# Selective-scan stage of a hybrid conv/attention network: carry handed to the scans by pointer, one pool of five state buffers, new orders on TensorE and ScalarE

## What is computed

```python
xs = jnp.stack([s0, s1, s0[..., ::-1], s1[..., ::-1]], axis=1)
x_dbl = jnp.einsum('bkdl,kcd->bkcl', xs, x_proj_w)
dts, bs, cs = (x_dbl[:, :, :R], x_dbl[:, :, R:R + N], x_dbl[:, :, R + N:])
dts = jnp.einsum('bkrl,kdr->bkdl', dts, dt_projs_w)
delta = jax.nn.softplus(dts + dt_projs_b[None, :, :, None])
def step(hst, inp):
    u_i, dt_i, b_i, c_i = inp
    dA = jnp.exp(dt_i[..., None] * A)
    hst = dA * hst + (dt_i * u_i)[..., None] * b_i[:, :, None, :]
    y = jnp.einsum('bkdn,bkn->bkd', hst, c_i)
    return (hst, y)
```

## Time and profile before

| what | value |
|---|---|
| median of 3 runs | 13091.68 us (13074.61 to 13094.74) |
| the profiled execution | 13113.0 us, span 13111.2 us |
| scan stage (first to last scan of VectorE) | 837.9 to about 11514 us |
| VectorE busy | 10558.8 us (81%) |
| GpSimd busy | 9200.7 us (70%) |
| TensorE busy, mean granted clock | 9546.4 us (73%), 0.816 |
| ScalarE busy | 9124.6 us (70%) |
| HBM | 148 GB/s over the span |

### The profile page before, as it was taken

One profiled execution on the slowest core, in us unless ns is written; L12 is line 12 of the kernel. 1 busy time (PEld: TensorE's weight loads), 2 busy tenths in 40 slices (PEclk: granted clock), 3 DMA queues, 4 the chain that ended last, 5 costly groups with the idle time before them and its releaser, 6 DMA issues. The chain is left out here.

```text
span 13111.2 us, 148286 instructions
## 1 busy us (share of the span) xinstructions
PE 9546.4 (73%) x34584; PEld 3395.6 (26%) x34584; DVE 10558.8 (81%) x6847; ACT 9124.6 (70%) x15557; POOL 9200.7 (70%) x3956
## 2 busy tenths in 40 slices
PE   8867676677777777766777776777767676669888
PEld 2322222222222222222222222222222222223333
DVE  6768888888888888888888888888888888866665
ACT  6767777777777777777777777777777777735555
POOL 0038888888888888888888888888888888822111
PEclk9977877778787877787878787888777888879998
DMA  3456666666666666666666666666666666644442
GB/s 101 127 138 159 158 161 160 163 160 159 153 159 163 161 156 160 158 162 160 163 156 161 159 155 163 161 160 157 159 161 160 163 163 163 160 109 104 102 101 52
DMA packets 577621, 1948.60 MB, mean 149 GB/s; under 512 B 106614, under 2 KB 111638, under 8 KB 562198
## 3 DMA queue, kind: packets, MB, share of 16 engines
q1 hardware_dynamic: 573714, 1938.65, 61.8%
q10 hardware_dynamic: 3076, 0.97, 0.0%
HBM read 1532.38 MB, written 406.85 MB: 148 GB/s over the span
## 5 line engine op out<-in xcount | busy, mean ns | idle before, releaser
L1057 POOL TENSOR_TENSOR dBu<-rep,shared 128x1024 f32<-128x1024 f32 x2304 | 5366.8, 2353 | 972.4 <-DMA rep<-dd_dram 866.6
L747 PE MATMUL py<-hC,fold 128*32 128x512 f32 x12288 | 2599.6, 766 | 1450.9 <-ACT y L917 1258.6
L1016 DVE TENSOR_TENSOR_SCAN pd<-pd,dBu 128x1024 f32<-128x1024 f32 x1536 | 3506.1, 2283 | 165.5 <-ACT dBu L851 138.7
L826 ACT ACTIVATE pd<-rep,a_now 128x1024 f32<-128x1024 f32 x2304 | 2560.9, 1112 | 354.4 <-DVE hC L1025 167.8
L1067 POOL TENSOR_TENSOR hC<-shared 128x1024 f32<-128x1024 f32 x768 | 1797.1, 2360 | 816.0 <-DVE shared L997 814.8
L1067 POOL TENSOR_TENSOR hC<-h,shared 128x1024 f32<-128x1024 f32 x768 | 1804.5, 2350 | 797.2 <-DVE h L1016 794.4
L1025 DVE TENSOR_TENSOR hC<-pd,shared 128x1024 f32<-128x1024 f32 x1536 | 1880.5, 1224 | 395.0 <-PE py L747 249.0
L1016 DVE TENSOR_TENSOR_SCAN h<-pd,dBu 128x1024 f32<-128x1024 f32 x768 | 1751.4, 2280 | 71.0 <-ACT dBu L851 49.1
L997 DVE TENSOR_TENSOR_SCAN shared<-shared,carry,pd 128x1024 f32<-128x1024 f32 x576 | 1319.2, 2330 | 522.9 <-PE pd L727 408.1
L883 ACT ACTIVATE shared<-shared,turned_b 128x192 f32<-128x192 f32 x4096 | 1551.7, 442 | 0.0
L747 PEld LDWEIGHTS py<-hC,fold 128*32 128x32 f32 x12288 | 493.9, 129 | 3262.0 <-issue 2957.0
(11 more groups left out here) (170 smaller groups left out, 12357.4 us busy)
## 6 DMA issues: line engine op xcount, KB each, us to landing
rep<-dd_dram SPq DMA_DIRECT2D x1024, 768.0 KB, 12.1
shared<-bc_dram SPq DMA_DIRECT2D x3584, 128.0 KB, 3.9
u<-u_dram SPq DMA_DIRECT2D x128, 768.0 KB, 5.8
dd_dram<-LG SPq DMA_DIRECT2D x256, 384.0 KB, 3.5
dd_dram<-RL SPq DMA_DIRECT2D x256, 384.0 KB, 3.7
y_dram<-y SPq DMA_DIRECT2D x256, 384.0 KB, 3.7
shared<-y_dram SPq DMA_DIRECT2D x63, 1536.0 KB, 16.0
u_dram<-shared SPq DMA_DIRECT2D x32, 1536.0 KB, 7.6
```

Source lines behind the costliest of these rows:

```text
L747: last = mm(py[32 * g:32 * g + 32, t2(t)], fold[:, :], hC[:, j % 2 * 3 + g, t2(t)], start=(j % 4 == 0), stop=(j % 4 == 3), skip_group_chec ...
L826: go(dst, rep[:, half, 0, g, :], ACT.Exp, scale=a_now[:, column(i)]).then_inc(S.exped, 1)
L1016: v.tensor_tensor_scan(turned(dst, k), turned(pd[:, i % 2, :], k), turned(dBu[:, ring(c, place(i)), :], k), 0.0, ALU.mult, ALU.add).then_i ...
L1057: nc.gpsimd.tensor_tensor(dBu[:, ring(c, p), :], rep[:, half, 1, g, :], BB[:, r, :], ALU.mult).then_inc(S.dbu, 1)
```

## The change

- All scans take `carry[:, i]` as their starting value; `fold_state`, 18 activations a chunk in three chunks of four, is gone with its semaphore.
- `hs` (3 places) and `h` (2) become one pool of five places for the 12 states that GpSimd weighs (`KEPT`), given out by the table `HOME`. A place is written when the tile that had it before has been weighed and saved.
- TensorE's order: `make_step(n + 2, 0)` now closes the body before (behind `make_x_dbl` and `turn_b`, ahead of reduce 7) where `make_step(n + 1, 0)` opened it; `add_up(n + 1, 0)` stands between reduce 0 and 1; `skip(n, 0)` moves from ahead of tile 9 to behind tile 14; reduce 2 stands between tiles 10 and 11; `make_step(n + 1, 1)` behind tile 14; reduce 6 ahead of `make_x_dbl`.
- ScalarE's tables are new: 12 steps of `scale_du` lie ahead in the chunk before (8 until now), `copy_b` moves to i = 23 of the chunk before, most steps of half 0 come one or two tiles earlier, `copy_y(n - 1, 1)` at i = 2, `copy_y(n, 0)` at i = 14, and `relu` and `one_plus` of half 1 right behind it.
- VectorE's `delta_u` moves from behind tiles 9 and 19 to behind tiles 10 and 20.
- `y` has one place for both halves, with one semaphore.

```diff
+        KEPT = tuple(i for i in range(NS) if TRIPLES[i // 3][1] == 3 or i % 3 == 2)
+        HOME = (0, 1, 2, 3, 4, 0, 1, 2, 3, 4, 2, 3)
...
+        def kept_before(n, i):
+            slot, at_slot = HOME[KEPT.index(i)], KEPT.index(i) - 1
+            while at_slot >= 0 and HOME[at_slot] != slot:
+                at_slot -= 1
...
@@ scan (VectorE)
+                    if is_kept(i):
+                        dve.wait_ge(S.hc_pool, done(weighed_pool(*kept_before(n, i))))
...
                 if c > 0:
-                    dve.wait_ge(S.folded, done(folds(bk, c, i)))
...
+                    dve.wait_ge(S.carried, done(carries(bk, c - 1, i)))
+                    first = carry[:, i:i + 1]
...
-                                     0.0, ALU.mult, ALU.add).then_inc(S.scanned, 1)
+                v.tensor_tensor_scan(turned(state(i), k), turned(decay, k), turned(drive, k),
+                                     first, ALU.mult, ALU.add).then_inc(S.scanned, 1)
@@ body (TensorE)
-                if left:
-                    make_step(n + 1, 0)
                 reduce_states(n, 0)
-                reduce_states(n, 1)
-                skip(n, s, 0)
                 if left:
                     add_up(n + 1, 0)
-                for i in (9, 10, 11):
-                    turn_back(bk, c, i)
+                reduce_states(n, 1)
+                turn_back(bk, c, 9)
+                turn_back(bk, c, 10)
                 reduce_states(n, 2)
+                turn_back(bk, c, 11)
                 turn_back(bk, c, 12)
                 if left:
                     turn_du(n + 1, 0)
                 turn_back(bk, c, 13)
+                turn_back(bk, c, 14)
                 if left:
                     make_step(n + 1, 1)
-                turn_back(bk, c, 14)
+                skip(n, s, 0)
                 reduce_states(n, 3)
...
                     turn_du(n + 1, 1)
+                reduce_states(n, 6)
                 if left >= 2:
                     make_x_dbl(n + 2, s)
-                reduce_states(n, 6)
-                if left >= 2:
                     turn_b(n + 2)
+                    make_step(n + 2, 0)
                 reduce_states(n, 7)
@@ tables and body (ScalarE)
-            AHEAD = 8
-            SCALE = {0: 4, 1: 3, 2: 3, 3: 1, 4: 2, 5: 3, 6: 4, 7: 4}
-            SCALE_NEXT = {21: 2, 22: 4, 23: 2}
+            SCALE = {0: 3, 1: 1, 3: 3, 4: 2, 5: 7, 6: 3, 7: 1}
+            SCALE_NEXT = {20: 3, 21: 3, 22: 1, 23: 5}
...
-                    if i + 2 < NS and c > 0 and not is_turned(i + 2):
-                        fold_state(bk, k, c, i + 2)
-                    elif i + 2 >= NS and c < NC - 1:
-                        fold_state(bk, k, c + 1, i + 2 - NS)
-                    if i == 3 and (c > 0 or k > 0):
+                    if i == 2 and (c > 0 or k > 0):
                         copy_y(n - 1, 1)
-                    if i == 15:
+                    if i == 14:
                         copy_y(n, 0)
```

More of the change, by code:

```diff
@@ L599, in store_y @@
                 sp.sem_inc(S.passed, 1)
-                sp.dma_start(a.y_flat[row, :, half, :], y[:, half, :]).then_inc(y_stored[half], 16)
+                sp.dma_start(a.y_flat[row, :, half, :], y[:, :]).then_inc(y_stored, 16)
             def load_first_y(n):
@@ L605, in load_first_y @@
                 sp.wait_ge(S.dbu_turned, done((n + 1) * TURNED))
-                for half in range(2):
-                    sp.wait_ge(y_stored[half], done(16 * K * NC))
+                sp.wait_ge(y_stored, done(32 * K * NC))
                 for k, sem in ((0, S.y_loaded0), (1, S.y_loaded1)):
@@ L660, in _ @@
             chunk_loop(sp, body)
-            for half in range(2):
-                sp.wait_ge(y_stored[half], done(16 * BK * NC))
+            sp.wait_ge(y_stored, done(32 * BK * NC))
         @block.tensor
@@ L717, in turn_back @@
                 n = bk * NC + c
[L718 to L723, removed]
+                pe.wait_ge(*freed(n, i))
+                if not is_kept(i - 2) and c < NC - 1:
+                    pe.wait_ge(S.carried, done(carries(bk, c, i - 2)))
                 for q in range(TB):
@@ L806, in expo @@
             def expo(bk, c, i):
-                n, i = at(bk * NC + c, i)
                 half, r, g = where(i)
+                n = bk * NC + c
                 if i % 12 == 0:
                     act.wait_ge(rep_loaded[half], done((n + 1) * 64))
[L811 to L819, removed]
-                else:
-                    if where(q)[1] < 3 and where(q)[2] < 2:
-                        act.wait_ge(S.hc_dve, done(weighed_dve(before, q)))
-                    else:
-                        act.wait_ge(S.scanned, done(scanned(before, q)))
+                if is_turned(i):
+                    act.wait_ge(S.hc_pool, done(weighed_pool(*kept_before(n, i))))
+                    for count in kept_carried(bk, c, i):
+                        act.wait_ge(S.carried, done(count))
+                    dst = kept(i)
+                else:
+                    act.wait_ge(*freed(n, i))
                     dst = pd[:, i % 2, :]
@@ L1016, in scan @@
-                v.tensor_tensor_scan(turned(dst, k), turned(pd[:, i % 2, :], k),
-                                     turned(dBu[:, ring(c, place(i)), :], k),
-                                     0.0, ALU.mult, ALU.add).then_inc(S.scanned, 1)
+                    decay, drive = kept(i), pd[:, i % 2, :]
+                else:
+                    dve.wait_ge(S.dbu, done(driven(n, place(i))))
+                    decay, drive = pd[:, i % 2, :], dBu[:, ring(c, place(i)), :]
+                    if is_kept(i):
+                        dve.wait_ge(S.hc_pool, done(weighed_pool(*kept_before(n, i))))
+                        for count in kept_carried(bk, c, i):
+                            dve.wait_ge(S.carried, done(count))
@@ L1034, in body @@
                 n, s = bk * NC + c, c % 2
-                for i in range(NS):
-                    scan(bk, k, c, i)
-                    if not is_turned(i) and i % 3 < 2:
-                        weigh(n, i)
-                    if i == 9 and left:
-                        delta_u(n + 1, 1 - s, 0)
-                    if i == 19 and left:
-                        delta_u(n + 1, 1 - s, 1)
+                for j in range(8):
+                    for i in range(3 * j, 3 * j + 3):
+                        scan(bk, k, c, i)
+                        if not is_kept(i):
+                            weigh(n, i)
+                        if left and i in (10, 20):
+                            delta_u(n + 1, 1 - s, (10, 20).index(i))
             chunk_loop(dve, body)
```

117 lines of the change are left out of this document (56 added, 61 removed).

## The result

The changed kernel takes 11,915.7 us (median of 4 runs, 11,912.25 to 11,927.4) against 13,093.2 for the kernel before (4 runs). The ratio is 0.9104, with a 95% interval of 0.9089 to 0.912. The forecast of 12,270 had the sign and lies 354 us too high; the measured time is inside the range and 81 us from rival (a), "nothing waits", which I had given 0.20. The gain was forecast at 6.3% and is 9.0%.

A forecast was written before the change was run, and what follows sets the result against it. VectorE was taken as the fullest engine, 71.0 us a chunk plus 12.4 of waits. Terms -187.8, -696.5, -314.4 (`copy_delta`), -249.0, +104, +64, +372, +84 sum to -824 us: 12,270 us, 6.3% faster; range 11,800 to 12,660.

The forecast's parts named there:

- rival (a): Nothing waits: TensorE stays fast and the late preparation chain and reduce 2 terms vanish; 11,835 us, chance 0.20.
- the pointer's +104: VectorE's scans: a carry by pointer instead of an immediate costs 60 ns in each of 1728 scans, +104 us.
- The waits that go: VectorE's waits for transposes, turned tiles' decays, delta copy, reduces and folds, each taken as an edit's target: 1447.7 us.
- Folds gone: VectorE's waits for ScalarE's folds all go, -187.8 us; the folds' own 607.4 us on ScalarE count nothing.
- Turned tiles: VectorE's waits for TensorE's transposes (629.1) and turned tiles' decays (67.4) go by new order and five places, -696.5 us.
- Reduce 2 ahead of tile 11: TensorE's reduce 2, newly ahead of tile 11's transposes, makes them late by 0.5 us a chunk, +64 us.
- Reduce 6: Placed ahead of `make_x_dbl` on TensorE, it no longer holds up the product of tile 0, -249.0 us.
- What is late next: Preparation chain round the chunk, from `copy_y` to `expo(3)`, makes scan 3 late by 3.0 us in 124 chunks, +372 us.
- Image ends: Reduce 7, queued behind `make_step`, delays ScalarE and SyncE's `load_rep`: 12 us at each of 7 image ends, +84 us.
- rival (d): Slower: TensorE falls to its low clock at the turned tiles, making later links late; 13,270 us, chance 0.05.
- Rival (b): GpSimd sets the pace, with 1 us of handing over in each of eight triples a chunk; 12,450 us, chance 0.10.
- (c): Turned tiles stay bound by just two PSUM places, half of the 696 us remains; 12,620 us, chance 0.08.

## Why the prediction was right, and where it was not

The sign and the main mechanism were right: the change takes VectorE's waits away, and a chunk comes close to its pace without them. That the time lies in the range is in part the range's width, for its low end is rival (a). Two of the signs named for "right" did not come: a chunk takes 74.2 us and not 76 to 78, and there is no new wait of 2 to 4 us once a chunk at tile 3.

- **"A chunk without a wait is thus 71.0 us", and the pointer's +104.** Right. A chunk of the change with all carries takes 72.1 us, which is 71.0 and 18 times 60 ns. The 60 ns are measured in the 1728 scans themselves.
- **The waits that go (-1447.7).** Right in size but for 22 us: the 314.4 for `copy_delta` still hold a second wait ahead of the first scan (21.7), so 292.8 were there to gain. The change has left 28 for transposes, none for delta, none for folds. Wrong in the account of who earns them. I gave each wait to the edit next to it. The runs show that they are not separate: taking away the folds alone brought 97 of their 188 us back as longer waits elsewhere and saved nothing, and the whole change but TensorE's order saved 120 us (ScalarE's tables 61 of them). The step that failed is "each of them is an edit's target".
- **"Folds gone: -187.8 ... counted at nothing" on ScalarE.** Wrong in both directions: worth 0 in the old orders, 492 in the new ones. The sentence that they "pay for the denser tables" was the true one; it should have had the price.
- **Turned tiles (-696.5).** For TensorE's part the mechanism was right: restoring the head of the chunk costs 753 us, restoring `make_step` 169. Together they are 922, above my 696: with the other waits ahead of it gone, VectorE waits 7 us at tile 9 where it waited 3.8. The part of the five places (67.4) was misread; these were waits for the transposes too. The 137 us from 922 to the 1059 of the whole order belong to the moves that no run took apart (half 0's `make_step`, reduce 2, reduce 7) or to what the moves do together.
- **Reduce 2 ahead of tile 11 (+64).** About right: the waits for transposes that are left are 21.4 + 6.9 us.
- **Reduce 6 (-249).** The wait went, but not through this edit: with reduce 6 back behind `make_x_dbl` the time is the same. TensorE waits less for u (2.36 us where the earlier trace rows have 5.90), and most of that came with ScalarE's tables.
- **"What is late next" (+372).** This is the term that did most to make the forecast 354 us too high: the waits that it stands for are 26 us at most (`DVE pd L1019 <- ACT pd L851`). The chain is real and nearly tight (3.4 us more in it gave 2.8 us of waits a chunk), but it is in time by 0.6 us, where I had it late by 3.0. The links as they ran in the change:

```profile
5506.05 1.02 ACT L926 ACTIVATE y<-py 96x1024 f32<-96x1024 f32 x1 [0.21 <-PE py L779]
...
5523.63 0.90 PE L747 MATMUL pp<-eye,RL 96*128 96x96 f32 x8 [2.67 <-DVE RL L1000]
5524.94 3.27 PE L779 MATMUL py<-hC,fold 128*32 128x512 f32 x12 [0.40 <-POOL hC L1068]
5528.14 3.62 PE L709 MATMUL pp<-u,w_x 96*38 96x512 f32 x8
...
5534.68 3.72 PE L727 MATMUL pp<-xdbl,w_dt 38*96 38x512 f32 x4 [0.81 <-ACT turned_b L872]
```

  The copy of y ends 3.5 us after the scan of tile 14 (at 5503.6), not 5. `make_x_dbl` starts 4.5 us after `turn_du`, not 6.7, because reduce 6 runs while u lands. It then takes 3.62 us, not 5.57, because reduce 6 stands right ahead of it and not an idle stretch. That is 5.7 us in three links, against 1.4 that the way from the copy to `turn_du` grew (15.2 to 16.6). I had noticed that the clock decides this term, and then chose by "the rows at low clock are the ones behind a wait, as here"; with reduce 6 moved ahead, `make_x_dbl` no longer was.
- **Image ends (+84).** Too much. The waits there were 11 us before and are 14 now, some 20 us over 7 ends.
- **Not in the sum:** the wait for reduce 3, 178 us. I had it only in rival (d), for all chunks or none. It comes in 35 of them. Without it, as with `skip` moved, the time would be below rival (a) and not 81 us above it. So a term that was too large and one that was missing met in the sum, which is luck as far as the number goes. The misses that the runs show, 346 (the chain), 64 (image ends) and 36 (reduce 2) too much against 178 and 22 too little, make 246 of the 354 us; the rest is not traced.
- **Rival (b)** is out: GpSimd is busy 94% of the stage, and VectorE's list has no row for a late `dBu`. The Trainium skill (GPSIMD Engine Reference, Key points) says that GpSimd contends with VectorE instructions that have two SBUF inputs. A pointer beside one tensor in SBUF shows next to nothing of it here: products of 2355 and 2362 ns against 2350 and 2360 before. For (c) the transposes wait 28 us, not 348.

## What to carry to other kernels

Waits in one loop over several engines are not a sum of prizes: take away one ahead of a later one and the later one can grow by as much. Find the place where the slowest engine meets the queue that sets it (here tile 9), ask what stands ahead of it in that queue that could have run earlier, and expect little from anything else until that is mended; freed time on a side engine gets its value only then. When a step may stand anywhere between two others, put it into an idle stretch of the queue and not next to the one that somebody waits for; on TensorE that can keep the clock up as well.

## What the runs showed of the hardware

- TensorE's clock decides single links by a factor of up to two, and the same instructions at the same place run at 1.00 in one chunk and 0.71 in another, although VectorE's scans of tiles 12 to 14, which set TensorE's pace there, take 6.71 us in both. A step of 1.9 us moved into the idle stretches ahead kept the clock at 0.95 or more in all chunks, where it had been low in 35.
- The place of a small step of TensorE changes the length of its neighbours: with reduce 6 ahead, `make_x_dbl` took 3.62 us and `make_step` 3.72 (means 3.75 and 3.47); with reduce 6 behind, 5.36 and 1.95 (means 5.89 and 1.97).
- A scan with its starting value behind a pointer takes 60 ns more than with an immediate, 2342 against 2282 ns for 1024 elements, whether it writes to PSUM or SBUF.
